# A factorization-machine tower on one core: row numbers loaded four tiles ahead, gathers waiting only for a free buffer, loops written out

## What is computed

```python
e = stack([tbl_0[ids[:, 0]], ..., tbl_38[ids[:, 38]]], axis=1)   # (2048, 39, 16)
x = e; outs = []
for W in (W0, W1):                       # (128, 39*39), (128, 128*39)
    inter = (x[:, :, None, :] * e[:, None, :, :]).reshape(B, last * 39, 16)
    x = einsum('bid,hi->bhd', inter, W)
    outs.append(x.sum(axis=-1))
h = concatenate([concatenate(outs, axis=-1), dense_ctx], axis=1)  # 272 columns
h = relu(h @ W_top1 + b_top1)            # 512
h = relu(h @ W_top2 + b_top2)            # 256
y = h @ W_top3                           # (2048, 1)
```

## Time and profile before

| | |
|---|---|
| median of 3 runs | 965.97 us (965.49 to 969.34) |
| span of the profiled execution | 1508.4 us |
| TensorE busy | 884.9 us |
| VectorE busy | 648.8 us |
| ScalarE busy | 600.9 us |
| GpSimd busy | 623.7 us |
| mean granted TensorE clock | 0.788 of full speed |

### The profile page before, as it was taken

One profiled execution on the slowest core, in us unless ns is written; L12 is line 12 of the kernel. 1 busy time (PEld: TensorE's weight loads), 2 busy tenths in 40 slices (PEclk: granted clock), 3 DMA queues, 4 the chain that ended last, 5 costly groups with the idle time before them and its releaser, 6 DMA issues.

```text
span 1508.4 us, 15925 instructions
## 1 busy us (share of the span) xinstructions
PE 884.9 (59%) x3824; PEld 686.1 (45%) x3824; DVE 648.8 (43%) x1012; ACT 600.9 (40%) x1033; POOL 623.7 (41%) x628
## 2 busy tenths in 40 slices
PE   0136393719268292763958367291863936629998
PEld 0014262508146181552846256270642724527886
DVE  2015292617155282442835156160632615427870
ACT  0013282407154171532735154160532714418772
POOL 6756437461714517154271715417054071450000
PEclk9997596759678596785977678595775967859999
DMA  4112142212122132122322122121221312203320
GB/s 130 24 39 61 38 113 52 69 45 66 26 75 61 23 98 68 38 52 51 85 59 58 27 77 71 39 67 25 78 59 18 95 27 70 67 13 101 106 78 3
DMA packets 101439, 88.81 MB, mean 59 GB/s; under 512 B 59925, under 2 KB 71325, under 8 KB 101250
## 3 DMA queue, kind: packets, MB, share of 16 engines
q1 hardware_dynamic: 81410, 83.02, 18.8%
q0 software_dynamic: 19968, 5.15, 3.9%
HBM read 21.35 MB, written 10.49 MB: 21 GB/s over the span
## 4 chain that ended last, share of the span: by engine, by line
PE 38%; another core or an unknown queue 28%; issue 20%; ACT 6%; DVE 4%; POOL 2%; DMA 1%; DVEq 0%; ACTq 0%; SPq 0%; POOLq 0%
PE mlp_ps L440 7%; PE g_ps L429 6%; PE x_ps L400 5%; PE x_ps L397 5%; PE x_ps L398 5%; PE rep_ps L386 3%; POOL e_rows L346 2%; ACT G L589 2%; PE mlp_ps L471 2%; PE mlp_ps L459 2%; DVE products L739 2%; ACT product_hi L572 2%; DVE product_lo L748 1%; PE aux_ps L368 1%
## 5 line engine op out<-in xcount | busy, mean ns | idle before, releaser
L346 POOL DMA_INDIRECT e_rows<-in_tbl_dram,ids_sb x624 | 623.5, 999 | 721.3 <-DMA ids_sb<-in_ids_dram 535.7
L748 DVE TENSOR_TENSOR product_lo<-products,product_hi 117x512 fp32r<-117x512 f32 (+1 forms) x448 | 308.1, 688 | 598.7 <-remote 369.6
L572 ACT CAST product_hi<-products 117x512 fp32r<-117x512 f32 (+1 forms) x448 | 281.4, 628 | 298.7 <-remote 131.2
L400 PE MATMUL x_ps<-product_lo,w_hi 117*128 117x512 f32 (+1 forms) x448 | 199.3, 445 | 176.0 <-issue 91.8
L397 PE MATMUL x_ps<-product_hi,w_hi 117*128 117x512 f32 (+1 forms) x448 | 254.7, 569 | 9.9 <-issue 9.9
L589 ACT COPY G<-g_ps 128x320 f32 (+1 forms) x256 | 189.4, 741 | 38.2 <-remote 24.6
L400 PEld LDWEIGHTS x_ps<-product_lo,w_hi 117*128 117x128 f32 (+1 forms) x448 | 92.5, 207 | 224.1 <-issue 104.5
L398 PE MATMUL x_ps<-product_hi,w_lo 117*128 117x512 f32 (+1 forms) x448 | 190.3, 425 | 0.0
L429 PE MATMUL g_ps<-e_diag,x1T_hi 128*128 128x320 f32 x512 | 134.7, 347 | 92.6 <-issue 58.9
L440 PE MATMUL mlp_ps<-G,w1T 128*128 (+1 forms) x624 | 186.8, 400 | 0.8 <-ACT G L589 0.8
L429 PEld LDWEIGHTS g_ps<-e_diag,x1T_hi 128*128 128x128 f32 x512 | 97.6, 206 | 126.9 <-issue 82.7
(11 more groups left out here) (42 smaller groups left out, 612.7 us busy)
## 6 DMA issues: line engine op xcount, KB each, us to landing
shifted<-cycle SPq DMA_DIRECT2D x128, 234.0 KB
left<-cycle SPq DMA_DIRECT2D x192, 78.0 KB
e_scratch<-e_parts SPq DMA_DIRECT2D x16, 640.0 KB
e_diag<-e_scratch SPq DMA_DIRECT2D x512, 20.0 KB
e_rows<-in_tbl_dram,ids_sb POOLq DMA_INDIRECT x624
shifted<-cycle SPq DMA_DIRECT2D x64, 156.0 KB
w1T<-in_L_rec_W_dram SPq DMA_DIRECT2D x1, 2496.0 KB
G<-in_L_rec_W_dram SPq DMA_DIRECT2D x1, 819.0 KB
```

Of the source, the lines that this page charges most:

```text
L346: nc.gpsimd.indirect_dma_start(out=e_rows[slot][:, f * D:(f + 1) * D], out_offset=None, in_=tables[f], in_offset=bass.IndirectOffsetOnAxis ...
L400: last = nc.tensor.matmul(x1_ps[c % 2][:, :], w0_hi[0:rows, k, :], product_lo[0:rows, (c * KT + k) % LO_RING, :], start=False, stop=(k == ...
L572: nc.scalar.copy(product_hi[0:rows, n % RING, :], products[0:rows, n % RING, :]).then_inc(hi_ready, 1)
L748: nc.vector.tensor_tensor(product_lo[0:rows, n % LO_RING, :], products[0:rows, n % RING, :], product_hi[0:rows, n % RING, :].bitcast(f32), ...
```

## The change

The row numbers get four buffers instead of two, and the load for tile t + 4 stands where the load for tile t + 2 stood (chunks 0 and 4). Four loads stand at the start instead of two. GpSimd waits for the row numbers of tile t and for the split of tile t - 2, as before, and no longer adds to the unused semaphore. The buffers of rows stay two (`SLOTS = 2`). The hardware loops of all five engines are written out in Python, so every wait value and address is a constant.

```diff
-        ids_sb = [sb(f"ids_sb{n}", [128, F], i32) for n in range(2)]
-        e_rows = [sb(f"e_rows{n}", [128, F * D]) for n in range(2)]
+        ids_sb = [sb(f"ids_sb{n}", [128, F], i32) for n in range(AHEAD)]     # AHEAD = 4
+        e_rows = [sb(f"e_rows{n}", [128, F * D]) for n in range(SLOTS)]      # SLOTS = 2
...
-            for slot in range(TPI):
-                sp.dma_start(ids_sb[slot][:, :], ids[slot * TB:(slot + 1) * TB, :]).then_inc(ids_loaded[slot], 16)
+            for t in range(AHEAD):
+                sp.dma_start(ids_sb[t][:, :], ids[t * TB:(t + 1) * TB, :]).then_inc(ids_loaded[t], 16)
...
-                    if c % CPT == 0 and not final:
-                        slot = c // CPT
-                        sp.wait_ge(gathered[slot], (it + 1) * (16 * F))
-                        sp.dma_start(ids_sb[slot][:, :], ids[bass.ds((it + 1) * NB + slot * TB, TB), :]).then_inc(ids_loaded[slot], 16)
+                    t = it * TPI + c // CPT
+                    if c % CPT == 0 and t + AHEAD < TILES:
+                        sp.wait_ge(gathered[t % SLOTS], (t // SLOTS + 1) * (16 * F))
+                        sp.dma_start(ids_sb[t % AHEAD][:, :], ids[(t + AHEAD) * TB:(t + AHEAD + 1) * TB, :]).then_inc(ids_loaded[t % AHEAD], 16)
...
-            def body(it):
-                for slot in range(TPI):
-                    pool.wait_ge(ids_loaded[slot], it * 16 + 16)
-                    after(pool, split_done, (it - 1) * TPI + slot + 1)
-                    pool.sem_inc(tiles_begun, 1)
-                    for f in range(F):
...
-            body(0)
-            with pool.Fori(1, ITERS) as it:
-                body(it)
+            for t in range(TILES):
+                pool.wait_ge(ids_loaded[t % AHEAD], (t // AHEAD + 1) * 16)
+                after(pool, split_done, t - SLOTS + 1)
+                for f in range(F):
...
-            with pe.Fori(2, ITERS - 1) as it:
+            for it in range(2, ITERS - 1):
...
-            with act.Fori(2, ITERS - 1) as it:
+            for it in range(2, ITERS - 1):
...
-            with dve.Fori(1, ITERS - 1) as it:
+            for it in range(1, ITERS - 1):
```

More of the change, by code:

```diff
@@ L38 @@
 ITERS = B // NB
+SLOTS = 2
+AHEAD = 4
 Q = COLS // 128
@@ L201, in cin_tower @@
         w0_split = sem("w0_split")
-        ids_loaded = [sem(f"ids_loaded{n}") for n in range(2)]
-        gathered = [sem(f"gathered{n}") for n in range(2)]
-        tiles_begun = sem("tiles_begun")
+        ids_loaded = [sem(f"ids_loaded{n}") for n in range(AHEAD)]
+        gathered = [sem(f"gathered{n}") for n in range(SLOTS)]
         e_hi_ready = sem("e_hi_ready")
@@ L326, in _ @@
             body(1, second=True)
-            with sp.Fori(2, ITERS - 1) as it:
+            for it in range(2, ITERS - 1):
                 body(it)
@@ L337, in _ @@
         def _(pool):
[L338 to L353 removed]
+            for t in range(TILES):
+                pool.wait_ge(ids_loaded[t % AHEAD], (t // AHEAD + 1) * 16)
+                after(pool, split_done, t - SLOTS + 1)
+                for f in range(F):
+                    nc.gpsimd.indirect_dma_start(
+                        out=e_rows[t % SLOTS][:, f * D:(f + 1) * D], out_offset=None, in_=tables[f],
+                        in_offset=bass.IndirectOffsetOnAxis(ap=ids_sb[t % AHEAD][:, f:f + 1], axis=0),
+                    ).then_inc(gathered[t % SLOTS], 16)
         @block.tensor
@@ L777, in chunk @@
                     if c == 2 and k == 1:
-                        split_hi(it * TPI + 1, it, 1)
+                        split_hi(it * TPI + 1)
                     if c == 2 and k == 2:
-                        split_lo(it * TPI + 1, 1)
+                        split_lo(it * TPI + 1)
                     if c == CPT + 2 and k == 1 and not final:
-                        split_hi(it * TPI + 2, it + 1, 0)
+                        split_hi(it * TPI + 2)
                     if c == CPT + 2 and k == 2 and not final:
-                        split_lo(it * TPI + 2, 0)
-            split_hi(0, 0, 0)
-            split_lo(0, 0)
+                        split_lo(it * TPI + 2)
+            split_hi(0)
+            split_lo(0)
             multiply(0, 0, 0)
```

14 lines of the change are left out of this document (5 added, 9 removed).

## The result

| | median, us | runs | against before |
|---|---|---|---|
| before | 965.73 (963.87 to 969.34) | 4 | 1 |
| the change | 975.73 (972.24 to 978.35) | 4 | 1.0104, 95% interval 1.0071 to 1.0136 |

The change is 1% slower. Forecast was no change, 965.0 us, with a range from 945 to 976.

What follows compares the result with a forecast made beforehand. GpSimd's gathers, back to back, were taken to bound the kernel. From 966.0 us, 1 us came off for GpSimd's loop and every other part counted 0, giving 965 us, no change, with a range from 945 to 976.

Steps and rivals of the forecast that it cites:

- What bounds the kernel: Whole kernel: GpSimd's gathers, back to back, set the time, with TensorE waiting some 4 us per tile at the split.
- T = 53.9 us per tile: Time of a tile's gathers beside VectorE's work, for fourteen tiles; the value the median of 966 us asks for.
- The part behind the last split: From the split of the last tile to the kernel's end: 108.4 us, read from the first profile.
- Four buffers, 0 us: Row-number buffers on GpSimd: two already deliver the numbers in time, so four save 0 us.
- GpSimd's loop, -1 us: Writing out GpSimd's loop removes a semaphore instruction per tile, register instructions and six branches back: 1 us saved.
- The four or five fetch stalls for its longer list: GpSimd's 462 added instructions might be fetched with stalls of 2.42 us, costing some 12 us; taken as 0.
- This is real work saved, but it lies on the side that waits: Five loop heads on VectorE and TensorE, 3.6 us each: 18 us saved on engines that wait for gathers.
- It only lengthens the wait at the split: 0 us: Writing out the loops of VectorE, TensorE, ScalarE and SyncE was priced at 0 us on the total time.
- VectorE starves GpSimd: Rival: without loop-head pauses a denser VectorE holds gathers up; 2.7 us for pauses, 23 with stopped gathers, 989 us; chance 0.12.
- The size of the interference: Gathers beside a busy VectorE: 0.12 to 0.15 us of excess per us of VectorE work, 40.5 us per tile.
- The range's upper end, 976: Denser VectorE raises the gathers' excess from 0.13 to 0.15 us per us over fourteen tiles: 11 us.
- What would show it: Expected profile signs: no 2.4 us VectorE gaps at five heads, GpSimd waiting for the split, gathers still 1.36 us and more.

Runs made afterwards that it cites:

- ring2_written_out: The kernel before with all loops written out and two buffers of row numbers kept; 983.31 us, 1.0157.
- only_pool_out: The kernel before with only GpSimd's loop written out; 968.49 us, 1.0012.
- the kernels with few gathers: The change and the kernel before, each with tiles 2 to 15 gathering 24 of 39 tables; 883.11 us (0.9118) and 897.29 us (0.9261).
- after_dve_loop: The change with VectorE's loop put back, the others written out; 969.92 us, 1.0009.
- after_all_sbuf: The change with products of steps 1 to 3 reading the cyclic buffer in SBUF instead of replicas in PSUM; 1021.02 us, 1.0562.
- before_again: The kernel before, unchanged, run for a second profile; 968.98 us, 1.0009, profiled span 962.4 us.

## Why the prediction was wrong

- **What bounds the kernel** was right, read against the profile's shares: gathers back to back, in an execution of 966 us and not of 1508. Predicted was T = 53.9 us per tile including the 0.3 us behind it; the tiles 2 to 15 of before take 53.11 + 0.31 = 53.4 and those of the change 53.85 + 0.31 = 54.2. The part behind the last split was 108.4 us, and 973.5 - 865.0 = 108.5 in the change. Only tile 1 was off: 52 us instead of 49.2.
- **Four buffers, 0 us**: right. ring2_written_out, without them, is 1.0157, no faster than the change.
- **GpSimd's loop, -1 us**: right within what can be measured (only_pool_out, 1.0012). The four or five fetch stalls for its longer list, put against it at 12 us, rested on no row, and the same run shows no sign of them.
- **"This is real work saved, but it lies on the side that waits"**, 18 us hidden: right as far as it goes. Uncovered, in the kernels with few gathers, it is 14.2 us instead of 18: a head costs 2.6 us and not 3.6.
- **"It only lengthens the wait at the split: 0 us" is the step that failed.** It priced VectorE's loop heads for the engines that wait, and put at nothing what they do to the gathers, although the text itself had found in the earlier trace rows that VectorE slows these. Measured are 10.5 us more of gathers, about 2.1 us for each of the five tiles across a head. The rival *VectorE starves GpSimd* had the place and the sign; it was put at 2.7 us for the pauses alone, at 23 us with whole gathers stopped, and given 0.12 because "the work on VectorE per tile does not change". Over an odd and an even tile that is true, 125 or 126 operations in both kernels, and still the pair takes 2.3 us longer (53.46 + 54.04 against 51.33 + 53.88). So the argument failed not in the amount of work but in taking the excess to follow from it.
- **The size of the interference**, 0.12 to 0.15 us of excess per busy VectorE us, fits three kinds of tile. With 39 x 1.249 - 0.31 = 48.4 us for undisturbed gathers, the even tiles 6 to 14 of before (mean 53.88 us, 42.4 us of VectorE) have 0.13, the odd and the even ones of the change (53.46 and 39.8; 54.04 and 40.3) 0.13 and 0.14. The tiles across a loop head have 2.9 / 37.25 = 0.08. The rate was carried over to them unchanged. The range's upper end, 976, was drawn from a rate that grows to 0.15 everywhere; that 975.73 lies just inside it is luck, since the growth is in the tiles across the heads alone.
- **What would show it** came as written for the gap at the heads, for the missing wait for row numbers, and for the span (it moved by 535 us, since the first one was odd). GpSimd was to wait for the split instead; it doesn't, since the split always waits for it.

What stays open is why a head of 2.4 us saves 2.1 us of gathers, when the two gathers that fit into it would save 1.1 at 0.55 each. Shown is that VectorE's loop does it, taken out alone and put back alone, and in these kernels mostly in the tiles across its head. Not separated are the pause at the head and the register instructions that the loop puts between VectorE's operations everywhere. A gather is due every 1.249 us and a pair of VectorE operations every 1.20, so the two drift slowly against each other, and a pause shifts them; that this is the way it acts is argued, not shown, and the count of starts by place in an operation doesn't support it across kernels. after_dve_loop (its odd tiles at 52.4, its ratio with the looping kernels) fits no simple rule.

No version that computes the same beat the kernel before.

## What to carry to other kernels

If a GpSimd queue of gathers sets the time, an edit on an engine "that waits anyway" isn't free when that engine's operations read SBUF beside the gathers: their number was the same here, so compare the summed time of the gathers, tile by tile, before and after. Writing out a loop pays on the engine that sets the time, and the same edit can be worth -14 us or +10 us depending on what binds; taking a third of the suspected work out of both kernels tells which in one run each. And when a profile's span is far from the timed median, profile again before arguing.

## What the runs showed of the hardware

- A gather of 128 rows of 64 bytes takes GpSimd 0.943 us and the next starts 0.305 us later. Beside VectorE operations with two SBUF inputs it took up to 6.32 us (after_all_sbuf); beside operations with one input in PSUM next to nothing was added (0.5 us over 138 gathers of the change).
- VectorE pays little. In the change 81 operations with two SBUF inputs start within 5 ns of a gather. In 51 cases the gather keeps its time and the operation takes 0.72 us instead of 0.69, and where the next follows at once it does so after 0.64 to 0.65 us instead of 0.60; in 30 the operation keeps its time and the gather takes 0.55 or 1.15 us more. One of the first kind, in before_again:

```profile
222.53 0.94 POOL L346 DMA_INDIRECT e_rows<-in_tbl_dram,ids_sb  x1 [0.31 <-issue]
...
222.53 0.72 DVE L748 TENSOR_TENSOR product_lo<-products,product_hi 117x512 fp32r<-117x512 f32 x1
223.17 0.68 DVE L739 TENSOR_TENSOR products<-shifted,left 78x512 f32<-78x512 f32 x1
```

- Halving VectorE's operations made the gathers 43 us longer in sum (713.1 against 669.8), not shorter: one of them passed none of ten boundaries between operations in a row.
- 40 memsets of one element took 0.61 us together, though each is shown with 59 ns: the duration of one small instruction is not its price in a row.
- One execution in the profile was 542 us longer than the median of the timed runs, with all engines halting and no releaser; the same kernel profiled again had none of it. What it was is not known.
